# GpSimd adds two pairs of weighed states in the layer-3 scan, and TensorE sums six buffers in place of eight

## What is computed

```
def step(h, inp):
    d_t, u_t, b_t, c_t = inp
    dA = jnp.exp(d_t[..., None] * A)
    h = dA * h + (d_t * u_t)[..., None] * b_t[:, None, :]
    y_t = jnp.einsum('bdn,bn->bd', h, c_t)
    return (h, y_t)
...
y = jnp.swapaxes(ys, 0, 1) + u * D_param
y = y * jax.nn.silu(z)
```

## Time and profile before

| what | value |
|---|---|
| median of three runs | 40388.22 us (40377.25 to 40404.15) |
| the profiled execution, its own time | 40396.46 us |
| its span, first to last instruction | 40394.6 us |
| DVE busy over the span | 33936.9 us (84%) |
| POOL busy | 30996.0 us (77%) |
| PE busy | 29251.1 us (72%) |
| ACT busy | 19958.1 us (49%) |
| mean granted TensorE clock | 0.875 |

### The profile page before, as it was taken

How to read it: one execution, slowest core, us unless ns; L and a number is a source line. 1 busy time by engine, 2 the same in 40 slices (tenths; PEclk the granted TensorE clock), 3 DMA queues, 4 the chain that set the end, 5 groups by cost and what they waited for, 6 DMA issues and landing times. The chain is left out here.

```text
span 40394.6 us, 270531 instructions
## 1 busy us (share of the span) xinstructions
PE 29251.1 (72%) x61476; PEld 11541.5 (29%) x61476; DVE 33936.9 (84%) x33869; ACT 19958.1 (49%) x37509; POOL 30996.0 (77%) x14776
## 2 busy tenths in 40 slices
PE   6777777777777777777777777777777777777777
PEld 3232232322323223232232322323223232232322
DVE  7969879698796987969879698796987969879698
ACT  4545545455454554545545455454554545545455
POOL 6949869498694986949869498694986949769497
PEclk8888888888888888888888888888888888888888
DMA  3424324243242432424324243242432424324243
GB/s 104 151 83 152 135 100 151 85 151 134 100 152 84 152 134 101 152 84 152 134 102 151 83 152 134 101 152 84 151 133 103 151 84 151 133 102 152 84 152 132
DMA packets 1387317, 5029.10 MB, mean 124 GB/s; under 512 B 164272, under 2 KB 165816, under 8 KB 1381440
## 3 DMA queue, kind: packets, MB, share of 16 engines
q1 hardware_dynamic: 1385536, 5010.20, 35.5%
HBM read 4938.25 MB, written 71.30 MB: 124 GB/s over the span
## 5 line engine op out<-in xcount | busy, mean ns | idle before, releaser
L662 PE MATMUL PS<-WORK,CST 128*128 128x512 f32 x36096 | 19792.8, 693 | 8395.9 <-POOL WORK L556 7606.2
L545 POOL TENSOR_TENSOR WORK<-WORK,XN 128x1024 f32<-128x1024 f32 x8192 | 19253.1, 2383 | 1.3
L662 PEld LDWEIGHTS PS<-WORK,CST 128*128 128x128 f32 x36096 | 7532.0, 220 | 20965.6 <-POOL WORK L556 10427.4
L1026 ACT ACTIVATE PS<-WORK,AN 128x512 f32<-128x512 f32 x17408 | 11307.0, 679 | 1984.9 <-DVE WORK L1576 1092.8
L1568 DVE TENSOR_TENSOR_SCAN PS<-PS,HST,WORK 128x512 f32<-128x512 f32 x8960 | 10975.2, 1272 | 45.4 <-ACT PS L1026 32.1
L1568 DVE TENSOR_TENSOR_SCAN WORK<-PS,HST,WORK 128x512 f32<-128x512 f32 x5376 | 6582.9, 1267 | 0.0
L556 POOL TENSOR_TENSOR WORK<-WORK,CWIDE 128x1024 f32<-128x1024 f32 x2048 | 4864.0, 2375 | 118.3 <-issue 65.2
L1026 ACT ACTIVATE HST<-PS 128x2 f32<-128x2 f32 x5152 | 858.6, 167 | 6586.2 <-DVE WORK L1576 6152.6
L632 POOL MEMSET XN<- 128x66 f32 x32 | 4.9, 154 | 5101.7 <-DVE SM L1414 5003.0
L1576 DVE TENSOR_TENSOR WORK<-PS,WORK 128x1024 f32<-128x1024 f32 x3072 | 3763.0, 1225 | 105.2
L1026 ACT ACTIVATE WORK<-PS 40x512 f32<-40x512 f32 (+2 forms) x1600 | 935.5, 598 | 3547.7 <-PE PS L662 2867.3
(11 more groups left out here) (158 smaller groups left out, 25260.5 us busy)
## 6 DMA issues: line engine op xcount, KB each, us to landing
XN<-xbc_rows SPq DMA_DIRECT2D x4096, 512.0 KB, 3.6
WORK<-xbc_rows SPq DMA_DIRECT2D x2816, 512.0 KB, 4.3
CWIDE<-xbc_rows SPq DMA_DIRECT2D x2304, 512.0 KB, 4.2
BIG<-in_spec_dram SPq DMA_DIRECT2D x32, 2048.0 KB, 12.3
X<-in_x_dram SPq DMA_DIRECT2D x68, 512.0 KB, 4.8
xbc_rows<-WORK SPq DMA_DIRECT2D x512, 64.0 KB, 3.1
out_dram<-X SPq DMA_DIRECT2D x64, 512.0 KB, 5.1
xbc_rows<-WORK SPq DMA_DIRECT2D x128, 32.0 KB, 1.6
```

What stands on the lines that cost most here:

```text
L545: nc.gpsimd.tensor_tensor(S.both(S.Q[u % 6]), S.both(S.DU[u // SN % 2]), S.wide(S.BW, u).unsqueeze(1).to_broadcast([P, 2, NT]), MUL).then_ ...
L662: return nc.tensor.matmul(o, w, r, start=start, stop=stop)
L1026: return nc.scalar.activation(o, i, f, **k)
```

## The change

After `weigh` of state 2 POOL adds the weighed state 1 to it, and after `weigh` of state 5 the weighed state 4 (`join`); PE skips `sum_up` of states 1 and 4. Waits that counted `summed` are recounted.

```
+            def joined(s, u):
+                return u % SN3 + 1 in s.pool
...
+            def wait_summed(s, e, u):
+                if s.joined(u):
+                    e.wait_ge(s.paired, s.pairs(u + 1))
+                else:
+                    e.wait_ge(s.summed, s.sums(u))
...
                     if u >= 6:
-                        e.wait_ge(S.summed, u - 5)
+                        S.wait_summed(e, u - 6)
...
+                def join(u):
+                    S.wait_weighed(e, u)
+                    S.wait_weighed(e, u - 1)
+                    nc.gpsimd.tensor_tensor(S.Q[u % 6], S.Q[u % 6], S.Q[(u - 1) % 6], ADD).then_inc(S.paired, 1)
...
                         if S.has(c) and S.on_pool(u):
                             weigh(u)
+                            join(u)
...
                     c, n = u // SN3, u % SN3
-                    S.wait_weighed(e, u)
+                    if S.joined(u):
+                        return
+                    if S.on_pool(u):
+                        e.wait_ge(S.paired, S.pairs(u))
+                    else:
+                        S.wait_weighed(e, u)
```

More of the change, by code:

```diff
@@ L207, in __init__, with sums, pairs @@
                 s.y_taken = sample_sem("s3_y_taken")
+                s.paired = sample_sem("s3_paired")
+            def joined(s, u):
+                return u % SN3 + 1 in s.pool
+            def sums(s, u):
+                return sum(not s.joined(v) for v in range(u + 1))
+            def pairs(s, u):
+                return sum(s.on_pool(v) for v in range(u + 1))
+            def wait_summed(s, e, u):
[3 more added lines that the diff above has]
+                    e.wait_ge(s.summed, s.sums(u))
             def on_pool(s, u):
@@ L1652, in take_y @@
                 def take_y(c):
-                    e.wait_ge(S.summed, SN3 * (c + 1))
+                    e.wait_ge(S.summed, S.sums(SN3 * (c + 1) - 1))
                     V.scalar_tensor_tensor(Y3[:, ch(c)], U3[:, ch(c)], vec["Dp3"], bank(0), MUL, ADD).then_inc(S.y_taken, 1)
```

## The result

The changed kernel takes 40536.76 us, the median of 8 runs (40494.08 to 40556.56), against 40390.98 us before: ratio 1.0035, 95% interval 1.0023 to 1.0046. It is slower by 146 us. The forecast was 40543 us. One of the eight runs of the kernel before fell in a slower state and took 41463.38 us; the ratio is taken without it.

The account below looks back on a forecast made before the run. No engine is full; a loop through DVE, ACT and PE bounds layer 3. 102 + 27 + 10 + 16 = 155 us on 40396.46 gives 40551, less 8 us for the median: 40543 us, range 40410 to 40635.

Parts of the forecast that it names:

- PE's saving is worth nothing on the path.: Two sums a chunk, 218 us in all, lie outside `rows` to `take_y`; ACT's chain covers them, gain 0.
- The pause grows to 3.1 to 4.3 us and brings half clock, 51 times 2.0 us, +102 us.: PE idle ahead of `rows`, chunks 2 to 5: 56 of 64 returns lost, 5 already before, 2.0 us each.
- a first pair of 1.9 in place of 1.02 us: Expected sign of half clock in PE's first pair behind the pause ahead of `rows`, with about 8 us to `take_y`.
- All five losses came in the longest: Argument against the clock holding: of 64 pauses ahead of `rows`, the five followed by half clock were the longest.
- Chunk 1, +27 us: `join` delays POOL's drive of state 5 and `sum_dt`, so ACT's table load comes 1.7 us later, 16 times.
- Chunks 2 to 6, 0 to 0.3 us: DVE's own work covers POOL's delay, by 0.2 us at state 5; 0.15 us for 80 chunks, +10 us.
- The last chunk, 1.0 us: No idle time at its `take_y`, so a late drive of state 0 reaches the image's end: 16 x 1.0, +16 us.
- both POOL terms: POOL's delay in chunks 2 to 6, +10 us, and in the last chunk, +16 us.
- The idle time at `take_y` up to about 780 us: Expected sign: DVE's total wait for PE at `take_y` rises from 678 us.
- The clock did not hold: Rival: PE keeps clock 1.00 behind 3.4 us pauses, leaving POOL's 53 us: 40441 us; chance 0.22.
- GpSimd as the bound everywhere: Rival: each `join` moves DVE or ACT, 2.7 us in all 128 chunks, +346 us: 40734 us; chance 0.05.
- PE as the bound: Rival: PE comes later than ACT at the last SiLU, each turn loses up to 1.70 us: 40279 us; chance 0.08.

Follow-up runs that it names:

- e2: The kernel before with PE's sums of states 1 and 4 left out and no addition on GpSimd, two states missing from y: 40499.72 us, ratio 1.0027.
- e1: The changed kernel with both joins, but TensorE repeats two products of the same size in each chunk: 40500.07 us, ratio 1.0028 to the kernel before.
- e8: The kernel before with both joins and the two missing TensorE sums in chunk 1 alone: 40473.34 us, ratio 1.0017.
- e3: The changed kernel with only the first pair (states 1 and 2) joined, states 4 and 5 summed by TensorE: 40493.43 us, ratio 1.0025 to the kernel before.
- e4: The changed kernel with only the second pair (states 4 and 5) joined: 40501.62 us, ratio 1.0026 to the kernel before.
- e9: The kernel before with ACT's SiLU of x2 moved from fourth to second place, so that `rows` can start sooner: 40397.67 us, ratio 0.9998.
- e5: The changed kernel with each addition on GpSimd behind the gate and next drive, not directly behind `weigh`: 40451.11 us, ratio 1.0014 to the kernel before.

## Why the prediction was right, step by step

- **PE's saving is worth nothing on the path.** Right: e2 has that saving alone and loses 108 us.
- **The pause grows to 3.1 to 4.3 us and brings half clock, 51 times 2.0 us, +102 us.** Right in kind, off in both factors. The pauses are 3.36 us in turns 2 to 4 and 5.1 in turn 1, above the forecast range there, and all 64 returns lost their clock, not 56. A loss costs 8.06 - 6.41 = 1.65 us in turns 2 to 4. The kernel before had lost it there already in one, one and three of 16 images, so the stretches grew by 1.55, 1.57 and 1.37 us on the mean, 72 us in all. The rest of these turns got shorter by 0.04, 0.13 and 0.14 us, since shorter waits for C rows outweighed the additions, so that they are 1.51, 1.44 and 1.23 us longer, 67 us. In turn 1 the stretch grew by 4.13 - 1.7 = 2.4 us, 39 us in all. That is 111 us for 59 losses, 1.9 us each, against 51 of 2.0. The mechanism was right; that the sum came so near is in part luck, as more losses met smaller ones. e1 and e2 show that it is the pause, and not the additions, in turns 2 to 4.
- **The sign "a first pair of 1.9 in place of 1.02 us".** Wrong in turns 2 to 4: in all 48 the first pair takes 1.02 to 1.19 us, since half clock sets in only behind it. The stretch of about 8 us came as forecast. In turn 1 the pair takes 1.90 us.
- **"All five losses came in the longest" pauses.** Not quite so. They came behind 1.83, 1.94, 2.20, 2.26 and 2.60 us, and seven pauses of 2.00 to 2.12 us kept the clock. The three longest of the 64 lost it.
- **Chunk 1, +27 us.** Right in its mechanism: 15.57 us from `take_y` to the table load in place of 13.88, 1.7 us. What I had not said is that these 1.7 us alone are enough for half clock behind them; turn 1 of e1 shows it, and 16 x 2.3 = 37 of the 60 us by which e1 was missed come from it. It was counted, since all four returns of an image were, but under the missing sums.
- **Chunks 2 to 6, 0 to 0.3 us.** Right: `sum_dt` ended 13.96 us behind `take_y`, forecast 14.0, and the scan of state 5 (2419.49) came 7.88 us behind it, just as before. The cover of 0.2 us at the scan held. Behind it the late `sum_dt` does cost, 0.24 us a turn by e2, near the 0.3 that I had for turns in which DVE does not wait for a C row: 12 us in turns 2 to 4 against 10 in the sum. In the time it is hidden behind the shorter waits for C rows.
- **The last chunk, 1.0 us.** Turn 6 is 1.15 us longer. But the stretch behind it is 0.96 us shorter, since all 16 images of the kernel before took 17.03 us or more there, five of them 18.4 to 18.7, against 16.57 in the changed one; I have not looked for the cause. This, with the first column and turn 5, leaves 11 us where I had 26 for both POOL terms. 67 + 66 + 11 = 144 us.
- **The idle time at `take_y` up to about 780 us.** Wrong: 653.8. I had added the clock's loss and forgotten that DVE, late by POOL's drives, arrives later at `take_y`. It changes nothing in the time, as the idle time only moved.
- **The rivals.** The clock did not hold in any of the 64. GpSimd as the bound everywhere is out by turns 2 to 4 of e1. PE as the bound is out by e2.

## What to carry to other kernels

An engine that waits once in each turn of a loop gives nothing back when its work is cut, and TensorE may take something: here 1.7 us less work in 26 us made the pause long enough for half clock behind it, on the path. Read the pauses ahead of TensorE's critical stretch, with the granted clock behind each, before taking work out, and sort all the cases by the length of the pause, those that kept the clock too. Where a loop is closed by two chains, price the second before expecting the gain of removing the first. Check too where each of them starts: what stands ahead of an instruction in its own engine's order can hold it as well as the data that it reads.

## What the runs showed of the hardware that was not expected

Half clock set in while PE was already busy again. In the 48 turns 2 to 4 of the changed kernel the first pair of `rows`, right behind the pause, still takes 1.02 to 1.19 us, and the slow products come behind it (2.07 us for the next pair in image 0).

The turns became very even. Before, the turns 2 to 4 of the 16 images were from 25.34 to 28.18 us; in the changed kernel all 48 lie between 27.22 and 27.35 us. This is not owed to half clock alone: turn 2 of e1 (25.57 to 25.59 us) and of e8 (25.34 to 25.36) is as even at full clock. In e3 the turns alternate in the same order in all images.

The length of the pause alone does not decide. Of two pauses of 2.27 us in e3 one was followed by a long turn and the other by a short one, in all 16 images; in e4 pauses of 2.26 to 2.48 us were followed by a long turn in 47 cases and, behind 2.27 us, by a short one in one. e9 kept the clock behind 2.36 us and lost it behind 1.85; e5 did both behind 1.32 to 1.35. What else decides, I have no run that shows.
